# Another order of routing, 4.5 shared pieces in front of the routed loop and 3.5 behind it, in a feed-forward, attention, feed-forward kernel

## The reference, cut to what matters

```
x = x + 0.5 * ffn(layernorm(x))
x = x + attn(layernorm(x))          # 32 query heads, 8 KV heads, head size 128, causal
x = x + 0.5 * ffn(layernorm(x))     # the same weights as the first

def ffn(x2):                        # 16 experts of 128, top 2; shared expert of 512
    g_s, u_s = split(x2 @ shared_w_gate_up.T)
    shared_out = silu(g_s) * u_s @ shared_w_down.T
    probs = softmax(x2 @ gate_w.T)
    vals, idx = top_k(probs, 2);  vals = vals / sum(vals)
    combine = sum(one_hot(idx, 16) * vals[..., None], axis=1)
    g, u = split(einsum('th,eih->eti', x2, w_gate_up))
    moe_out = einsum('eth,te->th', einsum('eti,ehi->eth', silu(g) * u, w_down), combine)
    return moe_out + shared_out
```

## Time and profile before

| | us |
|---|---|
| runs: median (lowest to highest) | 1189.51 (1187.71 to 1192.12), 3 runs |
| the profiled execution's own time | 1191.12 |
| its span | 1189.4 |
| PE busy | 1116.4 (94%) |
| DVE, ACT, POOL busy | 682.5, 568.4, 472.9 |
| chain that ended last, by engine | PE 83%, issue 5%, DVE 4%, ACT 2%, DMA 2%, POOL 1% |

### The profile page before, as it was taken

The page is one execution under the profiler, slowest core; times in us unless marked ns, Lnnn a source line. Parts: engine busy times, 40 slices in busy tenths (PEclk is TensorE's granted clock), DMA queues, the critical chain, the costliest instruction groups (busy, mean ns, idle before and its releaser), DMA issues.

```text
span 1189.4 us, 20230 instructions
## 1 busy us (share of the span) xinstructions
PE 1116.4 (94%) x5982; PEld 929.4 (78%) x5983; DVE 682.5 (57%) x1836; ACT 568.4 (48%) x1512; POOL 472.9 (40%) x485
## 2 busy tenths in 40 slices
PE   5989997689999999999999999999999989989995
PEld 4767775568888888888888888888888876867764
DVE  6767775765545445454545454554454456767766
ACT  3336661356536445444545553644553544246650
POOL 1265565225325323423432532532531410365545
PEclk9999999799999999999999999999999999999997
DMA  9975546200100010010010010110000017735446
GB/s 359 364 296 194 164 162 210 101 1 36 38 17 21 16 53 0 35 53 0 35 53 0 35 53 0 35 53 0 35 1 1 1 42 281 293 136 160 160 149 212
DMA packets 38603, 114.61 MB, mean 96 GB/s; under 512 B 4384, under 2 KB 4384, under 8 KB 36512
## 3 DMA queue, kind: packets, MB, share of 16 engines
q1 hardware_dynamic: 33440, 97.30, 22.4%
q0 software_dynamic: 5120, 16.78, 4.1%
HBM read 79.20 MB, written 34.87 MB: 96 GB/s over the span
## 4 chain that ended last, share of the span: by engine, by line
PE 83%; issue 5%; DVE 4%; ACT 2%; DMA 2%; POOL 1%; another core or an unknown queue 1%; DVEq 0%; SPq 0%; ACTq 0%; POOLq 0%
PE bank L1241 23%; PE bank L1310 15%; PE bank L1326 8%; PE bank L1276 8%; PE bank L1220 7%; PE bank L1254 6%; PE bank L1147 4%; PE bank L1228 4%; PE bank L1189 2%; PE bank L1163 2%; PE bank L1322 1%; POOL yg L488 1%; PE bank L1272 1%; PE bank L1208 1%
## 5 line engine op out<-in xcount | busy, mean ns | idle before, releaser
L502 POOL TENSOR_TENSOR scores<-scores,pinv 128x512 f32<-128x512 f32 (+3 forms) x256 | 176.5, 722 | 364.7 <-DVE pinv L1016 364.7
L454 POOL TENSOR_TENSOR tback_lo<-experts,tback_hi 128x768 fp32r<-128x768 f32 x62 | 114.9, 1854 | 75.2 <-ACT tback_hi L597 75.1
L683 ACT ACTIVATE scores<-scores,nmax 128x512 f32<-128x512 f32 (+3 forms) x256 | 140.4, 559 | 0.5 <-DVE nmax L1006 0.5
L657 ACT ACTIVATE pT_hi<-bank 128x512 fp32r<-128x512 f32 (+2 forms) x192 | 86.8, 487 | 107.8 <-PE bank L1254 107.8
L695 ACT ACTIVATE oT_hi<-bank 128x512 fp32r<-128x512 f32 x64 | 38.3, 598 | 207.7 <-PE bank L1322 207.7
L986 DVE TENSOR_TENSOR pT_lo<-bank,pT_hi 128x512 fp32r<-128x512 f32 (+2 forms) x192 | 100.8, 553 | 48.8 <-ACT pT_hi L657 48.8
L1006 DVE CUSTOM_DVE_ANT_0 scores<-bank,causal 128x512 f32<-128x512 f32 (+3 forms) x256 | 112.2, 486 | 1.5 <-issue 0.5
L1310 PE MATMUL bank<-wds_hi,oT_hi 128*128 128x512 f32 x256 | 105.3, 411 | 1.4 <-DVE oT_lo L990 1.4
L990 DVE TENSOR_TENSOR oT_lo<-bank,oT_hi 128x512 fp32r<-128x512 f32 x64 | 44.2, 691 | 108.6 <-ACT oT_hi L695 108.6
L1241 PE MATMUL bank<-xnT_hi,wqs_hi 128*128 128x512 f32 x256 | 105.9, 414 | 0.0
L1241 PE MATMUL bank<-xnT_hi,wqs_lo 128*128 128x512 f32 x256 | 101.7, 397 | 0.0
(11 more groups left out here) (197 smaller groups left out, 2933.9 us busy)
## 6 DMA issues: line engine op xcount, KB each, us to landing
experts<-in_ffn_w SPq DMA_DIRECT2D x32, 768.0 KB, 9.3
xn<-x_rows SPq DMA_DIRECT2D x62, 256.0 KB, 2.7
y_rows<-xn SPq DMA_DIRECT2D x62, 256.0 KB, 2.0
raw_q<-in_wq SPq DMA_DIRECT2D x8, 1024.0 KB
raw_d<-in_wd SPq DMA_DIRECT2D x8, 1024.0 KB
x_rows<-experts SPq DMA_DIRECT2D x1, 7936.0 KB, 29.7
raw_w<-in_ffn_w SPq DMA_DIRECT2D x8, 768.0 KB, 6.9
raw_kv<-in_wkv SPq DMA_DIRECT2D x8, 512.0 KB, 3.3
```

What stands on the lines that cost most here:

```text
L454: nc.gpsimd.tensor_tensor(tback[par][1][:], experts[:, bass.ds(at + FRONT, GU - FRONT)], tback[par][0][:].bitcast(F32), ALU.subtract).then ...
L502: nc.gpsimd.tensor_tensor(s, s, pinv[k % 2][:, i:i + 1].to_broadcast([P, P * (i + 1)]), ALU.mult).then_inc(att.normed, 1)
L657: nc.scalar.activation(pT[0][:, lo_col:hi_col], bank[b][:, 0:hi_col - lo_col], ACT.Copy).then_inc(att.t_hi, 1)
L683: nc.scalar.activation(s, s, ACT.Exp, bias=nmax[par][:, i:i + 1], scale=-1.0, accum_out=psumr[par][:, i:i + 1]).then_inc(att.exp, 1)
```

## The change

The router multiplies high and low gate weights side by side (32 rows) with the tokens' high part, and the high ones with the low part: 16 products instead of 24. The turn is now a product with `fold`, a 32 x 16 matrix of two identities, that adds both halves. The top two are taken from the logits; the weights come later from r = exp(l2 - l1). `place` comes right behind `router` on DVE and gives out `rows` before the table is made (`tabulate`). `rank` stands inside `gate_up(1)`. In front of the loop are pieces 0 to 3 and `gate_up(4)` with its Silu and multiply; half of `down(3)` stands before and half behind the first tile's turn. Part 3's weights are loaded at the end of the loop over the loop's tiles, its down weights have an own pair `wdn_late`. All low parts of the gate-and-up weights but part 0's are made on DVE. Behind the first feed-forward's loop, the cuts of attention's first weights are split among the pieces: on ACT behind pieces 5 and 6, on POOL one after each gather pair from tile 3 on. `wq` and `wd` are loaded without a wait for gathers. The adds of pieces 6 and 7 now wait for the combines of their tiles, where before combines waited for adds. The core of the diff:

```diff
-BEFORE = 6
+BEFORE = 4
-        gw = pair("gw", [P, HC, NEXP])
+        gw = sb("gw", [P, HC, 2, NEXP], F32R)
+        fold = sb("fold", [2 * NEXP, NEXP], F32)
-                raw_w = [sb(f"raw_w{p}", [P, FW], F32, sub) for p in range(2)]
+                raw_w = [sb(f"raw_w{p}", [P, FW], F32, sub) for p in (1, 0)][::-1]
+                sb("late_pad", [P, 2 * FW + 6 * 512], F32, sub)
+                wdn_late = pair("wdn_late", [P, HID], sub)
...
@@ sync
-                load_shared(n, 3)
 
                 sp.wait_ge(route[n].scattered, 2 * TT * 16)
...
                 for k in range(TILES % 4):
+                    if k == TILES % 4 - 2:
+                        sp.wait_ge(moe[n].gu_mm, TILES)
+                        load_shared(n, 3)
                     store_tile(n, last, k)
...
-            sp.wait_ge(gathered[HALF - 1], 2 * 16)
             sp.dma_start(raw_q[:], wq[0]).then_inc(loaded.q, 16)
             sp.dma_start(raw_d[:], wd[0]).then_inc(loaded.d, 16)
...
-                sp.wait_ge(moe[1].added, 4 * (t // 2) + 3 + t % 2)
                 sp.wait_ge(ffn[1].added, HALF * (SLOTS - 2) + t + 1)
@@ gpsimd
-                low_gu(n, NSH - 1)
+                pool.wait_ge(route[n].table, 1)
                 back(0, places(pool, 0)[0][1], 1)
-                low_dn(n, NSH - 1)
+                low_dn(n, BEFORE // 2)
...
                         ).then_inc(gathered[t], 16)
+                    if n == 0 and t >= HALF - 1:
+                        first_cuts(low_part, t - HALF + 1, t - HALF + 2)
...
-            pool.wait_ge(moe[0].y_mm, TILES)
-            first_cuts(low_part)
+            first_cuts(low_part, HALF + 1)
@@ scalar, feed_forward
                 shared(n, 0, 1)
                 router(n)
-                shared(n, 1, BEFORE)
+                shared(n, 1, 2)
+                weigh(n)
+                shared(n, 2, BEFORE)
+                gate(n, BEFORE)
                 routed(n)
-                shared(n, BEFORE, SLOTS)
+                high(n, BEFORE)
+                shared(n, BEFORE + 1, SLOTS - 2)
+                if n == 0:
+                    act.wait_ge(loaded.kv, 16)
+                    first_cuts(high_part, 0, 2)
+                shared(n, SLOTS - 2, SLOTS - 1)
+                if n == 0:
+                    act.wait_ge(loaded.q, 16)
+                    first_cuts(high_part, 2)
+                gate(n, SLOTS - 1)
+                if n == 0:
+                    roots(1, 0)
+                high(n, SLOTS - 1)
@@ vector, router
-                then(nc.vector.tensor_reduce(lmax[:], logits, AX_X, ALU.max))
-                nc.vector.tensor_tensor(lsub[:], logits, lmax[:].unsqueeze(2).to_broadcast([P, TT, NEXP]),
-                                        ALU.subtract).then_inc(s.sub, 1)
-                dve.wait_ge(s.exp, 1)
...
+                then(nc.vector.tensor_copy(scores[:], logits))
...
+                nc.vector.tensor_tensor(below_top[:], top8[:, :, 1], top8[:, :, 0], ALU.subtract).then_inc(s.sub, 1)
@@ vector, place
+                then(nc.vector.tensor_scalar(ntile[:], total, 1.0 / P, (P - 1) / (2.0 * P), ALU.mult, ALU.add))
+                then(nc.vector.tensor_scalar(ntile[:], ntile[:], ROUNDED, -ROUNDED, ALU.add, ALU.add))
...
+                nc.vector.tensor_copy(rows[:].rearrange("p t m -> p m t"), rowf[:]).then_inc(s.rows, 1)
+
+            def tabulate(n, then):
...
+                then(nc.vector.tensor_copy(tile_w[:], wordf[:]))
+                dve.wait_ge(s.exp, 1)
+                then(nc.vector.tensor_scalar(tsum[:], ratio[:], 2.0, 2.0, ALU.mult, ALU.add))
+                then(nc.vector.reciprocal(wtop[:, :, 0], tsum[:]))
+                nc.vector.tensor_tensor(wtop[:, :, 1], wtop[:, :, 0], ratio[:], ALU.mult).then_inc(s.table, 1)
@@ vector, add_down
-                    if s == SLOTS - 2 and t < 2:
-                        dve.wait_ge(moe[n].added, 3 + t)
+                    if s >= SLOTS - 2:
+                        dve.wait_ge(moe[n].added, 8 * (s % 2) + 4 * (t // 2) + 3 + t % 2)
@@ vector, feed_forward and behind it
                 then = router(n)
+                place(n, then)
                 shared(n, 1, 2)
-                place(n, then)
+                tabulate(n, then)
                 shared(n, 2, BEFORE)
+                multiply(n, BEFORE)
                 routed(n)
-                shared(n, BEFORE, SLOTS - 1)
+                low(n, BEFORE)
+                shared(n, BEFORE + 1, SLOTS - 1)
                 combine(n, 0)
-                shared(n, SLOTS - 1, SLOTS)
                 combine(n, 2)
 
             feed_forward(0)
-            normalise(1, 0)
+            add_down(0, SLOTS - 2)
+            then = statistics(1, 0)
+            multiply(0, SLOTS - 1)
+            scaled(1, 0, then)
+            low(0, SLOTS - 1)
             turned_norm(1, 0)
-            add_down(0, SLOTS - 1)
             combine(0, 4)
             combine(0, 6)
+            add_down(0, SLOTS - 1)
             attention()
             feed_forward(1)
-            add_down(1, SLOTS - 1)
+            multiply(1, SLOTS - 1)
+            low(1, SLOTS - 1)
+            add_down(1, SLOTS - 2)
             combine(1, 4)
             combine(1, 6)
+            add_down(1, SLOTS - 1)
@@ tensor, feed_forward
                 down(n, 0)
-                rank(n)
                 for s in range(2, BEFORE):
                     gate_up(n, s)
                     down(n, s - 1)
-
+                gate_up(n, BEFORE)
+                pe.wait_ge(route[n].table, 1)
+                down(n, BEFORE - 1, range(0, HALF // 2))
+                pe.wait_ge(ffn[n].mul, BEFORE + 1)
                 turn(n, 0, 0, 0, 1)
-                down(n, BEFORE - 1)
+                down(n, BEFORE - 1, range(HALF // 2, HALF))
                 routed(n)
...
+                gate_up(n, BEFORE + 1)
+                pe.wait_ge(moe[n].y_out, TILES)
+                down(n, BEFORE)
+                gate_up(n, BEFORE + 2)
+                down(n, BEFORE + 1)
+                if n == 0:
+                    down(n, SLOTS - 2)
+                    gate_up(n, SLOTS - 1)
+                    turn_norm(1, 0)
+                else:
+                    gate_up(n, SLOTS - 1)
+                    down(n, SLOTS - 2)
                 down(n, SLOTS - 1)
```

More of the change, by code:

```diff
@@ L175, in build @@
         loaded = sems("loaded", "x0 x1 x2 x3 gate q kv d")
-        consts = sems("consts", "mem ident below earlier counts zero causal0 causal")
+        consts = sems("consts", "mem ident below earlier counts fold zero causal0 causal")
         NORMS = 3
@@ L432, in _ @@
                                     pattern=[[1, NEXP], [-1, NEXP]], channel_multiplier=0).then_inc(consts.earlier, 1)
+            for m in range(2):
+                wait(pool, consts.fold, m)
+                nc.gpsimd.affine_select(out=fold[:], in_=fold[:], compare_op=ALU.not_equal, fill=1.0, base=-m * NEXP,
+                                        pattern=[[-1, NEXP]], channel_multiplier=1).then_inc(consts.fold, 1)
             nc.gpsimd.tensor_copy(counts[:], counts_i[:]).then_inc(consts.counts, 1)
@@ L558, in cut_dn, with gate, high @@
                 f = ffn[n]
-                wait(act, f.d_mm, 4 * 2 * e)
-                nc.scalar.activation(wdn[0][:], raw_w[e % 2][:, GU:FW], ACT.Copy).then_inc(f.dn_hi, 1)
+                if e < NSH - 1:
+                    wait(act, f.d_mm, 4 * 2 * e)
+                nc.scalar.activation(down_weights(e)[0][:], raw_w[e % 2][:, GU:FW], ACT.Copy).then_inc(f.dn_hi, 1)
+            def gate(n, s):
+                f = ffn[n]
+                act.wait_ge(f.g_mm, s + 1)
+                wait(act, f.act_lo, s - 1)
+                if s == 1:
+                    act.wait_ge(route[n].turned, 1)
+                nc.scalar.activation(sg[s % 2][:], bank[s % 2][:], ACT.Silu).then_inc(f.silu, 1)
+            def high(n, s):
+                f = ffn[n]
+                act.wait_ge(f.mul, s + 1)
+                wait(act, f.d_mm, 4 * (s - 1))
+                nc.scalar.activation(ab[s % 2][0][:], sg[s % 2][:], ACT.Copy).then_inc(f.act_hi, 1)
             def shared(n, first, last):
-                f = ffn[n]
                 for s in range(first, last):
-                    par = s % 2
-                    act.wait_ge(f.g_mm, s + 1)
-                    wait(act, f.act_lo, s - 1)
-                    if s == 1:
-                        act.wait_ge(route[n].turned, 1)
-                    nc.scalar.activation(sg[par][:], bank[par][:], ACT.Silu).then_inc(f.silu, 1)
+                    gate(n, s)
                     if s % 2 and s // 2 + 1 < NSH:
                         cut_gu(n, s // 2 + 1)
-                    act.wait_ge(f.mul, s + 1)
-                    wait(act, f.d_mm, 4 * (s - 1))
-                    nc.scalar.activation(ab[par][0][:], sg[par][:], ACT.Copy).then_inc(f.act_hi, 1)
-                    if s % 2 == 0 and s and s != BEFORE:
-                        cut_dn(n, s // 2)
+                    if s == SLOTS - 3:
```

(19 more changed lines are left out.)

142 lines of the change are left out of this document (64 added, 78 removed).

## The result

| | before | after |
|---|---|---|
| median of 4 runs, us | 1189.08 (1187.71 to 1192.12) | 1181.18 (1178.88 to 1182.96) |
| profiled execution, its span | 1191.12, 1189.4 | 1182.96, 1181.3 |
| PE busy, granted clock | 94%, 0.982 | 95%, 0.985 |

A forecast was written before the change was run, and what follows sets the result against it. TensorE, busy 94% of the span, was taken as the bound. First feed-forward 15.0 - 0.3 - 0.2 = 14.5 us, second 13.3 - 0.3 - 6.3 = 6.7, together 21.2 saved: median 1168, range 1160 to 1178.

The forecast's parts named there:

- Piece 1 starts 1.1 earlier: First front, behind the router: eight fewer matmuls save 1.9 us of PE, but piece 1 starts only 1.1 us earlier.
- `rank` at 34.6: First front: PE reaches `rank` at 34.6 us, after 18 of piece 1's 24 products.
- 30.4, 34.6 and 39.8: First front, forecast times in us: piece 1 starts at 30.4, `rank` at 34.6, first scatter at 39.8.
- `rank` to rows to first scatter, 5.2 us: First front: `rank` from 34.6 to 36.5, `rows` ready at 39.5, scatters start at 39.8 us, 9.7 earlier.
- 0.3 us a front for DMA contention: Both fronts: loads and earlier scatters share the DMA engines; 0.3 us lost in each, 0 to 1.5 if shared evenly.
- rival 3: Rival, chance 0.08: loads hold the earlier scatter for half of its 9.7 us in both fronts; 12.4 us more, 1180.
- PE waits 1.0 for the first tile, then full clock: First front's end: PE waits 1.0 us, turns two tiles around half a down, starts the loop's products at 67.8.
- Second front 13.3: Second feed-forward, before its loop: the loop starts 13.3 us earlier, 11.2 of work moved and 2.1 won.
- Expert 3's late load, DVE's tight steps: First tail: shared expert 3's later load stays hidden; first front: DVE's `low_gu` and `low_dn` steps are tight but hidden.
- First tail -0.2: First loop's end to attention's first score product: 1.4 us gained, 1.6 lost to POOL subtracts blocking DVE; net -0.2.
- Second tail 6.3: Last loop's end to the span's end: DVE's longer row of work makes it 6.3 us longer.
- Of the rivals, 1: Rival, chance 0.18: DVE-bound tails cost more, by POOL subtracts met, half clock and expert 3's load; 7.6 more, 1176.

The follow-up runs named there:

- 32-wide turn: Changed kernel with the scores turned by 32-wide transposes instead of `fold` products, DVE adding the halves: 1176.76 us (0.9886); 1195.76 (1.0018) in a later comparison.
- the pause: Changed kernel plus twelve POOL memsets after ten of sixteen transfers, in second front and second tail: 1185.78 us (0.9946); with the 32-wide turn 1183.83 (0.9945).

## Why the prediction was wrong, step by step

- **Piece 1 starts 1.1 earlier** (first front): failed, and with it `rank` at 34.6. "8 x 0.23 of PE go" was right; that `fold` products cost what transposes cost was taken without looking. They are two entries each (1.9 us a front instead of the 0.8 of 32-wide transposes), and the low clock behind them, where it comes, costs 1.5 to 2.7 us up to `rank`. Shown by the 32-wide turn, which meets 30.4, 34.6 and 39.8. The second front's piece 0 lost another 1.9 us: 0.4 are the turn itself at low clock, 1.5 a low clock ahead of it, whose cause is open (seen in the second front of five of the eight `fold` profiles, and of one of the eight with transposes).
- **`rank` to rows to first scatter, 5.2 us**: right (37.68 to 42.91).
- **0.3 us a front for DMA contention**: 1.1 us in the first, none in the second, and by another mechanism. The sum took bytes over 410 GB/s; what sets the landing, here as in the kernel before, is POOL's row of 16 instructions, which grew by 1.1 us where DVE's two-input operations ran beside it. A late landing behind that row, rival 3's mechanism, is seen at 0.3 to 1.8 us in five of 18 profiles, none of them the changed kernel's own.
- **PE waits 1.0 for the first tile, then full clock**: 2.0 us, and clock 0.63 behind it: 3.34 us where 2.1 were counted. The hole of the earlier trace rows did not go, it is half as long.
- **Second front 13.3**: 8.1. The turn and the low clock behind and ahead of it, as above; with 32-wide transposes it is 13.9, in a profile that also had no low clock ahead of the turn.
- **Expert 3's late load, DVE's tight steps**: hidden, as said.
- **First tail -0.2**: -2.7. Of the 3.8 us bound for the locks 3.7 were met, where 1.6 were taken. That the first score product would come earlier without them is argued, not shown.
- **Second tail 6.3**: 6.6. Right.
- Of the rivals, 1 held in its first part, the locks. That 1181 lies by rival 3's 1180 is chance: the loads did not hold the scatter. What none had is ACT held while POOL streams: in other comparisons it makes the changed kernel 16 to 17 us slower (12 to 14 beyond what the kernel before moved) and turns the whole into 0.3 to 0.4% slower. The change exposes it: where PE waited 8.0 us in the second front, the held Silu is one that its next piece needs, while the kernel before had ACT waits that PE never waited for.

Open: what holds ACT and why only in some comparisons. That a break in POOL's stream frees it is shown, by two kernels in one comparison and by the unbroken first front of each.

The best measured version is the changed kernel with the 32-wide turn: 1176.76 where nothing is held, 1195.76 where it is; with the pause 1183.83 there. Where ACT is held, the turn gave 1.6 and 2.0 us (1197.31 against 1195.76, 1185.78 against 1183.83), differences within the intervals.

## What to carry to other kernels

A product that replaces a transpose must be priced by its own rows: the new router saved 1.9 us of products, and `fold` cost 1.0 itself and up to 2.7 at the lower clock behind it. When a chain is pulled forward, ask of each transfer at its end what limits it: here it was POOL's 16 instructions, at 1.26 us each and more beside DVE, and not the bytes. And work that is moved beside a long POOL stream of indirect transfers is worth a second comparison at another time, with a pause in the stream as the trial.

## What was not expected of the hardware

- The same program took 1181 us in one comparison and 1197 to 1198 in two others, while the kernel before moved by 3 to 4 us only. ACT stood in waits of up to 12 us while POOL issued indirect transfers back to back, and went on inside a pause of 3.1 us.
- Products of 128x512 between the `fold` products did not keep the granted clock up: 0.76, then 0.50, though PE was busy throughout.
- POOL's scatters took up to 1.87 us each beside DVE operations with two SBUF inputs, instead of 0.96, and so set when the tiles land.
